# At most two row scatters in flight in the two mixture layers of a decoder kernel

## The reference

```
# layer 0: 16 experts of inner width 352, gated, 6 of them per token; a shared expert of width 704
topk_idx, topk_weight = _gate(layernorm(x))                  # (1024, 6)
comb = zeros((T, E)).at[arange(T)[:, None], topk_idx].add(topk_weight)
for e in range(16):
    out = out + comb[:, e:e+1] * ((silu(hs @ gate[e].T) * (hs @ up[e].T)) @ down[e].T)
x = x + out + (silu(hs @ sg.T) * (hs @ su.T)) @ sd.T
# layer 1: 8 experts of inner width 352, not gated, 2 of them per token; a shared expert of width 352
for e in range(8):
    routed = routed + comb[:, e:e+1] * (silu(xf @ w1[e]) @ w2[e])
x = x + silu(xf @ w_shared1) @ w_shared2 + routed
```

## Time and profile before

| | busy us | share of the span |
|---|---|---|
| TensorE matmuls | 1842.6 | 89% |
| VectorE | 1111.7 | 54% |
| GpSimd | 1001.5 | 49% |
| ScalarE | 788.0 | 38% |

### The profile page before, as it was taken

One profiled execution on the slowest core, in us unless ns is written; L12 is line 12 of the kernel. 1 busy time (PEld: TensorE's weight loads), 2 busy tenths in 40 slices (PEclk: granted clock), 3 DMA queues, 4 the chain that ended last, 5 costly groups with the idle time before them and its releaser, 6 DMA issues.

```text
span 2063.0 us, 30652 instructions
## 1 busy us (share of the span) xinstructions
PE 1842.6 (89%) x10235; PEld 1599.9 (78%) x10241; DVE 1111.7 (54%) x2750; ACT 788.0 (38%) x2029; POOL 1001.5 (49%) x964
## 2 busy tenths in 40 slices
PE   6999899753999999799769999999999999988796
PEld 4888777543899898699657888888887888876685
DVE  5666875451333333233656666666666667455244
ACT  3766542200222222122146556656564433213231
POOL 3434431584383759891736645456453003007584
PEclk8999999976999999999989999999999999889898
DMA  3556320353353445532433333233321210003465
GB/s 105 166 159 191 135 104 1 114 195 121 114 204 118 156 166 184 190 123 71 139 97 98 98 87 90 63 94 98 82 69 43 65 46 21 1 29 115 147 222 180
DMA packets 102693, 232.32 MB, mean 113 GB/s; under 512 B 18816, under 2 KB 19072, under 8 KB 99472
## 3 DMA queue, kind: packets, MB, share of 16 engines
q1 hardware_dynamic: 82224, 144.11, 23.1%
q0 software_dynamic: 19744, 85.47, 12.1%
q10 hardware_dynamic: 576, 0.79, 0.1%
HBM read 126.23 MB, written 57.93 MB: 89 GB/s over the span
## 4 chain that ended last, share of the span: by engine, by line
PE 70%; DVE 6%; POOL 6%; another core or an unknown queue 4%; DMA 3%; ACT 3%; issue 3%; SPq 3%; ACTq 0%; DVEq 0%; POOLq 0%
PE bank L149 57%; PE bank L957 3%; PE bank L941 2%; PE bank L2049 2%; PE bank L2040 2%; DMA a_g<-a_f 2%; SPq L620 2%; SPq L605 1%; POOL a_g L651 1%; POOL f_UL L161 1%; DMA a_QL<-a_g 1%; PE bank L327 1%; POOL a_E L657 1%; PE bank L938 1%
## 5 line engine op out<-in xcount | busy, mean ns | idle before, releaser
L657 POOL TENSOR_SCALAR a_E<-a_E,a_inv 128x128 f32<-128x128 f32 (+3 forms) x384 | 219.8, 590 | 222.4 <-DVE a_inv L792 222.4
L149 PE MATMUL bank<-f_UH,f_XH 128*128 x596 | 201.4, 338 | 22.1 <-POOL f_UL L161 16.4
L690 ACT ACTIVATE a_E<-a_E,a_top 128x512 f32<-128x512 f32 (+3 forms) x384 | 211.2, 567 | 7.8 <-DVE a_top L786 7.7
L149 PE MATMUL bank<-f_UL,f_XH 128*128 x596 | 193.6, 325 | 0.0
L149 PE MATMUL bank<-f_UH,f_XL 128*128 x596 | 193.4, 325 | 0.0
L682 ACT ACTIVATE a_PHL<-bank 128x512 fp32r<-128x512 f32 (+1 forms) x288 | 130.9, 528 | 132.8 <-PE bank L957 132.8
L149 PE MATMUL bank<-a_PHL,a_VH 128*128 128x512 f32 (+3 forms) x768 | 180.8, 324 | 0.3 <-DVE a_QL L161 0.3
L786 DVE CUSTOM_DVE_ANT_0 a_E<-a_causal,bank 128x512 f32<-128x512 bf16 (+3 forms) x384 | 163.8, 482 | 30.6 <-PE bank L941 19.0
L1708 DVE TENSOR_TENSOR f_gate<-bank,f_gate 128x352 f32<-128x352 f32 x79 | 41.4, 524 | 251.0 <-PE bank L149 209.7
L1651 ACT ACTIVATE f_HH<-bank 128x256 fp32r<-128x256 f32 x220 | 60.0, 325 | 301.9 <-PE bank L2040 223.3
L149 PE MATMUL bank<-f_DH,f_HH 128*128 (+1 forms) x330 | 141.0, 427 | 32.1 <-DVE f_HL L161 26.3
(11 more groups left out here) (397 smaller groups left out, 5054.6 us busy)
## 6 DMA issues: line engine op xcount, KB each, us to landing
f_uraw<-f_up POOLq DMA_DIRECT2D x18, 1408.0 KB, 6.3
f_xb<-table SPq DMA_DIRECT2D x86, 256.0 KB
table<-f_ob SPq DMA_DIRECT2D x86, 256.0 KB
table<-a_zeros SPq DMA_DIRECT2D x31, 512.0 KB, 4.4
f_draw<-f_down POOLq DMA_DIRECT2D x27, 512.0 KB
a_g<-a_f SPq DMA_DIRECT2D x160, 64.0 KB, 2.0
a_raw<-a_qkv SPq DMA_DIRECT2D x36, 256.0 KB, 3.4
f_uraw<-f_up POOLq DMA_DIRECT2D x9, 704.0 KB, 4.5
```

The costliest lines, as they stand in the source:

```text
L149: m = pe.matmul(out, a, b, start=first and i == 0 and j == 0, stop=last and i == n - 1 and j == 2, skip_group_check=not check)
L657: e.tensor_scalar(self.E[sl][:, a], self.E[sl][:, a], self.inv[:, sl, i:i + 1], 0.0, ALU.mult, ALU.add).then_inc(*self.s_nrm.up(N, m - 1, i))
L690: x = e.activation(E, E, ACT.Exp, scale=-1.0, bias=self.top[:, sl, i:i + 1], accum_out=self.total[:, sl, i:i + 1])
```

## The change

Scatters alternate between two semaphores instead of having one per choice. Before scatter i of choice j GpSimd waits for the scatter two before it to land. The waits of SyncE and of the early gathers are rewritten for these semaphores: they wait for the last two scatters of the choice. Apart from this, every value that is read from memory into a register to be waited for goes through one more instruction that makes it at least 1, on GpSimd and on TensorE.

```
-        self.s_sent = [sig(f"sent{j}") for j in range(6)]
+        self.s_sent = [sig(f"sent{x}") for x in range(2)]
...
-            self.s_sent[j].plan((N,), 16 * NT)
+            for i in range(NT):
+                self.s_sent[i % 2].plan((N, j, i), 16)
...
                 if i < self.top:
-                    e.wait_ge(*self.s_sent[i].after(N))
+                    for t in (NT - 2, NT - 1):
+                        e.wait_ge(*self.s_sent[t % 2].after(N, i, t))
...
             for i in range(NT):
+                if i >= 2:
+                    e.wait_ge(*self.s_sent[i % 2].after(N, j, i - 2))
+                elif j:
+                    e.wait_ge(*self.s_sent[i % 2].after(N, j - 1, NT - 2 + i))
                 e.indirect_dma_start(out=self.k.table[0:self.NR * P, :],
                                      out_offset=bass.IndirectOffsetOnAxis(ap=self.idx[:, j, i:i + 1], axis=0),
-                                     in_=self.rows[i], in_offset=None).then_inc(*self.s_sent[j].up(N))
+                                     in_=self.rows[i], in_offset=None).then_inc(*self.s_sent[i % 2].up(N, j, i))
...
-                e.reg_load(regs, self.ends[0:1, w - 4:w - 4 + n])
+                self._load_bounded(e, self.k.pool_loaded[0:n], regs, self.ends[0:1, w - 4:w - 4 + n])
...
-                for j in range(self.top):
-                    e.wait_ge(*self.s_sent[j].after(N))
+                for t in (NT - 2, NT - 1):
+                    e.wait_ge(*self.s_sent[t % 2].after(N, self.top - 1, t))
                 self._gather_early(0)
...
-        e.reg_load([reg], self.ends[0:1, self.R + j:self.R + j + 1])
+        self._load_bounded(e, self.k.pool_loaded[0:1], [reg], self.ends[0:1, self.R + j:self.R + j + 1])
...
+    def _load_bounded(self, e, loaded, to, of):
+        e.reg_load(loaded, of)
+        for reg, x in zip(to, loaded):
+            e.reg_alu(reg, x, 1, ALU.max)
...
-            e.reg_load(self.k.pe_registers[i // 8 % 2][0:min(8, self.NR - i)], self.owner[0:1, i:i + min(8, self.NR - i)])
+            m = min(8, self.NR - i)
+            self._load_bounded(e, self.k.pe_loaded[0:m], self.k.pe_registers[i // 8 % 2][0:m], self.owner[0:1, i:i + m])
```

More of the change, by code:

```diff
@@ L110, in constants @@
         self.table = self.nc.dram_tensor("table", [tiles * P, D], F32).ap()
+        self.pe_loaded = [self.pe.alloc_register(f"loaded{i}") for i in range(8)]
         self.pe_registers = [[self.pe.alloc_register(f"tile{g}_{i}") for i in range(8)] for g in range(2)]
+        self.pool_loaded = [self.pool.alloc_register(f"expert_loaded{i}") for i in range(4)]
         self.pool_registers = [self.pool.alloc_register(f"expert{i}") for i in range(5)]
```

## The result

The changed kernel takes 2022.08 us (median of 4 runs, 2019.72 to 2025.42), the kernel before 1998.38 beside it (4 runs, 1996.85 to 1999.92): ratio 1.0124, 95% interval 1.0103 to 1.0146, so 23.7 us slower. The forecast was 9 us slower, about 2008 us, in a range that ended at 2018. The profiled execution took 2019.72 us, with a span of 2018.2.

The account below looks back on a forecast made before the run. TensorE carries 70% of the chain of waits, with the profile's stops taken out. Longer scatter chains add 7.2 us in the first mixture and 1.9 in the second, 9.1 on 1998.75: about 2008 us, range 1997 to 2018.

Parts of the forecast that it names:

- The subtraction: Profiled span 2063.0 us less 68.1 of stops gives 1994.9; 3.9 us around it make the median.
- this stop: TensorE, ScalarE and VectorE nearly idle from 443 to 478 us during first-mixture scatters; claimed to belong to the profiled execution.
- rival A: Stops are real and fewer scatters in flight end them: 50 us faster, 1949 us, if all goes; chance 0.14.
- the pair: Two scatters from start to restart on GpSimd: claimed 2.80 us against 2.53, so first mixture +6.2 us, second +1.9.
- tile loads: Five 256 KB loads among first-mixture scatters, each holding up a pair: not charged, 5 x 0.5 us at the upper end.
- The pair of 3.56 us: Alternative from the Trainium skill's DMA rule, counted from the end of issuing: first mixture 23.7 us more; set aside.
- The path: Last scatter, landing, load, TensorE's transposes of tile 5 (first mixture) and tile 1 (second): delays paid in full, +7.2 and +1.9.
- Registers: One more ALU instruction per loaded register, 86 on TensorE and 25 on GpSimd: claimed hidden, 0 us.
- GpSimd's weights: Expert 3's weights, queued behind GpSimd's scatter waits, ready at about 514 instead of 506 us: nothing charged.
- Rival C: Landing slower once issues wait, or tile loads and clock add up: +34 us, 2033 us; chance 0.11.
- Rival B: Without profiling a scatter lands in under 2.4 us, so waits never end late: about 1999.5 us; chance 0.20.
- The sentence on instruction fetches: On the stop from 443 us: no instruction packets from 441 to 512 us, so the trace disagrees with a starved fetch.

Follow-up runs that it names:

- e1: The kernel before with only the bounded register loads, no wait between scatters: 1997.46 us, ratio 0.9999 to the kernel before.
- e9: The changed kernel with eight scatters in flight in the first mixture and two in the second: 2061.31 us, ratio 1.0006 to the kernel before.
- e10: The changed kernel with four scatters in flight on four semaphores instead of two: 2067.28 us, ratio 1.0016 to the kernel before.
- e14: The changed kernel once more, on the chip of e9 and e10: 2035.16 us beside 2054.59 for the kernel before, ratio 0.9891.
- e5: The changed kernel with SyncE's first tile load waiting for the last scatter of its mixture: 2052.83 us, ratio 1.0284 to the kernel before.
- e4: The changed kernel with one scatter in flight instead of two: 2111.42 us, ratio 1.0574 to the kernel before.
- e6: The changed kernel with one GpSimd wait for all choices' routing, ahead of the third scatter: 2020.28 us, ratio 1.0116 to the kernel before.

## Why the prediction was wrong

**What bounds the kernel: right for the timed chips, wrong in its reason.** The subtraction (2063.0 less 68.1) gave 1994.9 for a span without stops; e1 has 1995.5, and its wait of 2.53 us before tile 5 is the forecast's 2.5. (The 3.9 us "around it" were what was left over; the runs have 1.2 to 1.6.) But "I take this stop to belong to the profiled execution" was false. The arithmetic showed only that the timed runs had no stop. It couldn't tell a cost of profiling from a profile taken on another chip, and the latter is what e9 and e10 point to (which chip the profile of before ran on is not recorded). Against rival A I had also set that two in flight are "hardly less" than 2.15; e14 shows that this was no argument.

**The step that failed** is the pair and what is added to it: 23 x 2.80 and +1.0, 7.2 us, where the first mixture took 20.4:

| term, f0 | forecast | measured |
|---|---|---|
| 23 undisturbed pairs, against 2.53 | 23 x 0.27 = 6.2 | 23 x 0.45 = 10.4 |
| first two landings, behind the weights | 1.0 | 1.5 |
| tile loads, with the store and the packet that e5 also lacks | 0, up to 2.5 in the range | 5.4 (changed less e5) |
| second wait at a change of choice | none | 5 x 0.47 = 2.4 |
| e5's one late landing, beside an instruction packet | none | 1.0 |
| sum | 7.2 | 20.7 (20.4 seen) |

The landing was right to 0.03 us. GpSimd's waking of 0.26 stood in the earlier trace rows, and their sum, 2.99, was my upper bound of an undisturbed pair; 2.98 is what the changed kernel has. I took 2.80 with no row for it, between the two bounds. That cost 4.1 us. (The pair of 3.56 us that stands beside the forecast as an alternative, with 23.7 for f0, comes nearer to the 20.4 only by chance: an undisturbed pair is 2.98.) The other 9 us are disturbances: nothing waits for them scatter by scatter in a free stream, and a throttled one adds them up. I had named the loads and called 5 x 0.5 the end; with what came beside them they were 5 x 1.1. Nor are the 1.5 us the weights' alone: two instruction packets stand in f0's first landing (431.3 and 432.7 us), which takes 4.02 us, while in f1, where none does, the first takes 3.03. In f1 the same terms make 5.9 to 6.3 instead of 1.9: 7 x 0.45 = 3.2, the load and what left with it 2.2, the rest 0.9.

**The path was right**: nothing hides the scatters, the wait for tile 4 lies within that for tile 5, nothing gives the time back. **Registers** cost nothing (e1). **GpSimd's weights** cost nothing that shows: in the changed kernel the only wait of TensorE that the profile lists from 515 to 600 us is the one for tile 5, and in e4, where the weights start 87 us later, the loss is still the chain's. **Rival C**, slow landings and loads, was the nearest of my cases in mechanism, and priced at 34 it was too dear. **Rival A** is true of one chip of the seven that the experiments ran on, at -19 us (-26 against the 2061.22 of the other comparison there) rather than -50: the 58.9 us that the stops of both mixtures cost, less 26.3, would be 33, and three pieces of 3 to 4 us beside gathers remain in e14. **Rival B** is out.

The sentence on instruction fetches went too far as well. The Trainium skill, "Runtime: NRT & Kernel Launch", section on instruction fetch, says that each sequencer drives a DMA queue of its own to fetch its instructions, by which the stop could be a starved fetch. I wrote that the trace disagrees. From 441 to 512 us the profile of before has no instruction packet at all, e9 has one (at 511.3, behind its stop), e14 two, and e1:

```profile
q8 instruction: 4, 0.07, 0.4%
```

That TensorE went on at 477.85 and ScalarE at 498.23 without a packet speaks against a fetch, of those that the profile records, as what ended the stop. But a stop without packets is also what starving would look like, and what engines that consume no instructions would look like, and no row tells whose instructions come over which queue. So these rows decide neither way. The waits of the kernel before from 443 to 500 us have ScalarE and VectorE halted:

```profile
ACT f_HH L1651 <- remote: 45.8, 1, 45.8
...
PE bank L2040 <- issue: 34.0, 1, 34.0
DVE f_gate L1708 <- remote: 33.5, 1, 33.5
DVE X L1750 <- remote: 19.1, 1, 19.1
...
PE bank L149 <- DVE f_HL L161: 9.2, 1, 9.2
```

TensorE comes behind them: its 34.0 us are put down to "issue", but these transposes (L2040) read what VectorE's L1708 has written, and start at 477.85, 0.05 us after it has ended. What holds the two, and why on that chip alone, stays open.

## What to carry to other kernels

A throttle on DMAs in flight turns the mean rate into landing plus waking, and every late landing into lost time: count the loads, weights and second waits that fall among them, and take the sum of the rows, not a value between the bounds. Three in flight cost about a fifth of what two did; four, measured only on the chip with the stop, nothing that could be told. When a profile's span doesn't fit the timed runs, don't explain it away: ask which chip it ran on, because this change lost 1% on the others and gained 1% on that one.

## What the runs showed of the hardware

- A scatter of 128 rows of 2 KB lands 2.70 to 2.72 us after its start, with one in flight as with two; GpSimd wakes 0.27 us later, 0.74 where it has a second wait to go through, and 0.27 again without that wait (e6).
- A 256 KB load of SyncE beside such scatters makes a landing 4.1 to 4.5 us where it starts 0.6 us behind the scatter, 3.0 to 3.2 where it starts 0.2 ahead, and leaves it at 2.7 to 2.8 where it starts 0.7 ahead or 1.0 behind (nine profiles; not tested by itself).
- TensorE's granted clock is 0.80 over the 8.3 us behind the wait for tile 5 in the changed kernel, 1.00 in e1, which takes 6.7 us for the same work.
- On one of the seven chips of the experiments ScalarE and VectorE halt for up to 43 us (e9), and TensorE with them, while scatters are issued freely or four deep (e10: up to 30); with two in flight they don't (e14). The profile of before, whose chip isn't recorded, has 46.
